# Scores of two heads at once in the two 64-row halves of TensorE, and fillers in one piece

## What is computed

```python
q = (x @ Wq)                       # 32 heads of 16 columns
k, v = x @ Wkv                     # 8 groups; each is shared by 4 heads
scores = q @ k.T                   # per head 1024 x 1024, causal
weights = softmax(scores / 4)      # HD = 16, so 1 / sqrt(HD) is 1/4
x = layernorm(x + (weights @ v) @ Wo + bo)
h = x @ lora_A.T ; lora = h @ (lora_B * coef)      # 8 adapters of rank 16
out = layernorm(x + x @ W.T + bias + lora)
```

## Time and profile before

| | us |
|---|---|
| median of 3 runs | 341.34 |
| lowest and highest | 339.17, 341.63 |
| the profiled execution, whole | 339.0 |
| its span in the trace | 337.2 |

### The profile page before, as it was taken

How to read it: one execution, slowest core, us unless ns; L and a number is a source line. 1 busy time by engine, 2 the same in 40 slices (tenths; PEclk the granted TensorE clock), 3 DMA queues, 4 the chain that set the end, 5 groups by cost and what they waited for, 6 DMA issues and landing times.

```text
span 337.2 us, 7240 instructions
## 1 busy us (share of the span) xinstructions
PE 322.3 (96%) x2487; PEld 169.7 (50%) x2487; DVE 256.6 (76%) x787; ACT 216.5 (64%) x418; POOL 135.3 (40%) x268
## 2 busy tenths in 40 slices
PE   8999989999999999999999999999999999999992
PEld 3676445455353344454444544544544434558882
DVE  3557968978888899888889889888886961047664
ACT  4754737645657796848757668478585786952431
POOL 8845325433547585347222123212141122331553
PEclk9999999999999999999999999999999999999998
DMA  6886494874244120020010100000000000000002
GB/s 202 289 163 170 132 183 120 225 230 118 53 148 155 36 63 5 3 47 3 3 48 33 48 4 3 0 31 3 3 0 3 32 2 1 2 33 1 0 33 93
DMA packets 16643, 22.96 MB, mean 68 GB/s; under 512 B 3232, under 2 KB 10560, under 8 KB 16608
## 3 DMA queue, kind: packets, MB, share of 16 engines
q1 hardware_dynamic: 16608, 22.51, 24.4%
HBM read 16.29 MB, written 6.03 MB: 66 GB/s over the span
## 4 chain that ended last, share of the span: by engine, by line
PE 71%; DMA 7%; DVE 7%; ACT 4%; issue 4%; SPq 3%; POOL 2%; POOLq 0%; DVEq 0%; ACTq 0%
PE PS L1337 18%; PE PS L1195 16%; PE PS L1135 15%; PE PS L1359 15%; DMA QS<-NMR 3%; ACT PB L856 2%; PE PS L1263 2%; PE PS L1255 2%; DVE scrap L917 2%; DVE MX L910 2%; DMA scr_q<-parts 2%; DMA X<-in_L_attn_x_turned_dram 1%; SPq L490 1%; PE PS L1149 1%; SPq L502 1%
## 5 line engine op out<-in xcount | busy, mean ns | idle before, releaser
L856 ACT ACTIVATE PB<-PS 128x512 f32<-128x512 f32 x288 | 155.6, 604 | 59.1 <-PE PS L1359 57.9
L917 DVE CUSTOM_DVE_ANT_0 scrap<-PS,mask 128x128 bf16<-128x128 f32 (+3 forms) x256 | 111.5, 487 | 17.6 <-PE PS L1135 17.1
L1135 PE MATMUL PS<-KS,QS 96*128 96x512 bf16 (+3 forms) x384 | 107.9, 329 | 2.1 <-DVE MX L910 1.0
L1359 PE MATMUL PS<-QS,KS 99*128 99x512 bf16 x288 | 106.2, 381 | 1.8 <-DMA QS<-NMR 1.4
L910 DVE TENSOR_REDUCE MX<-PS 128x1 f32<-128x512 f32 x128 | 81.9, 684 | 12.4 <-PE PS L1135 11.7
L696 POOL TENSOR_SCALAR_AFFINE_SELECT PB<-PB 128x256 f32<-128x256 f32 (+1 forms) x96 | 46.4, 485 | 104.3 <-ACT PB L856 101.2
L1337 PE MATMUL PS<-PB,VX 128*32 128x256 f32 (+1 forms) x1280 | 78.8, 364 | 0.6 <-ACT PB L856 0.3
L1135 PEld LDWEIGHTS PS<-KS,QS 96*128 96x128 bf16 x384 | 32.9, 98 | 49.4 <-issue 13.6
L1337 PEld LDWEIGHTS PS<-PB,VX 128*32 128x32 f32 x1280 | 33.5, 109 | 41.9 <-issue 19.0
L1195 PE MATMUL PS<-XT,WQ 128*128 128x512 f32 x144 | 45.4, 439 | 0.5 <-ACT NMR L744 0.4
L1359 PEld LDWEIGHTS PS<-QS,KS 99*128 99x128 bf16 x288 | 27.5, 98 | 31.4 <-ACT PB L856 7.9
(11 more groups left out here) (93 smaller groups left out, 263.6 us busy)
## 6 DMA issues: line engine op xcount, KB each, us to landing
scr_q<-parts SPq DMA_DIRECT2D x8, 384.0 KB, 4.0
QS<-scr_q SPq DMA_DIRECT2D x15, 192.0 KB, 2.9
X<-in_L_attn_x_turned_dram SPq DMA_DIRECT2D x8, 256.0 KB, 6.3
X<-in_L_attn_x_dram SPq DMA_DIRECT2D x8, 256.0 KB, 3.1
out_dram<-TC SPq DMA_DIRECT2D x8, 256.0 KB, 2.0
QS<-scr_q SPq DMA_DIRECT2D x15, 128.0 KB, 3.0
RAW<-in_L_attn_Wo_dram SPq DMA_DIRECT2D x2, 512.0 KB, 5.9
RAW<-in_L_ffn_W_dram SPq DMA_DIRECT2D x2, 512.0 KB, 9.0
```

What stands on the lines that cost most here:

```text
L856: nc.scalar.activation(PB[:, cyc % NP_BUF, k, :], PS[:, score_bank(e), :], ACT.Exp, scale=SCALE)\
L917: last = nc.vector.tensor_tensor_reduce(out=scrap[:, n % 2, (j - j0) * width:(j - j0 + 1) * width], in0=bank[:, j - j0, :], in1=mask[:, HT ...
L1135: last = nc.tensor.matmul(PS[:, CHUNK_BANK[n], k * width:(k + 1) * width], QS[0:ROWS, u % SLOTS, j, qb * P:(qb + 1) * P], KS[0:ROWS, g, k0 ...
L1359: nc.tensor.matmul(PS[:, score_bank(e), :], KS[0:NROW, u % G, kb * P:(kb + 1) * P], QS[0:NROW, u % SLOTS, heads[0]:heads[-1] + 1, s * HQ + ...
```

## The change

The parts of q and k become two float32r values (high and low) instead of three bfloat16, and a score is three products (48 rows of the array). With the three rows of the maxima that is 51 rows, under 64. So rows 0 to 63 of the array take heads 0 and 1 of a unit, and rows 64 to 127 heads 2 and 3, each with its own keys: the heads are dealt anew, so that a unit has two heads of each of two groups (`v_group`). The two matmuls of a pair have different rows of the array and different PSUM banks, stand behind each other in the queue of PE, and only the second raises the semaphore.

- Scores for exp: a cycle has two `pair_scores` (quarters 0 and 2) instead of four or three `piece_scores`. Both banks must be free before the first matmul. The diagonal has four pieces (two of 256 columns) and four masks.
- Maxima: chunks come in pairs, with both banks free before the first matmul. The planner deals pairs over quarters.
- Fillers, long and short, are issued whole in quarter 3, after its chunks and before `accumulate`.
- ACT has no middle part (L737), POOL and DVE no low third part (L582, L968). `direct` has 2 products instead of 3 and two query matmul groups instead of four.
- The rows of unit 0 go the same way as the others, by `turn_maxima` and a DMA. A unit's rows take two DMAs instead of three, its queries four instead of three, the keys four instead of six.

The core of the diff:

```diff
-    ROWS = 6 * HD
+    ROWS = 3 * HD
     NROW = ROWS + NPART
+    PAIR, TILE = 2, 64
+    Q_TERMS, K_TERMS = (0, 0, 1), (0, 1, 0)
...
-        return first + ([(1, range(0, 4), P)] if on_diagonal(cyc) else [(1, heads, 0) for _, heads, _ in first])
+        return first + [(1, heads, P if on_diagonal(cyc) else 0) for _, heads, _ in first]
...
-        QS = sb("QS", [P, SLOTS, REP, HT], BF16)
-        KS = sb("KS", [P, G, T], BF16)
+        QS = sb("QS", [P, SLOTS, NPAIR, HT], F32R)
+        KS = sb("KS", [P, G // 2, T], F32R)
...
                 was_read(CHUNK_BEHIND[n])
-                for k, j in enumerate(heads):
-                    last = nc.tensor.matmul(PS[:, CHUNK_BANK[n], k * width:(k + 1) * width],
-                                            QS[0:ROWS, u % SLOTS, j, qb * P:(qb + 1) * P],
-                                            KS[0:ROWS, g, k0:k0 + width], start=True, stop=True)
+                was_read(CHUNK_BEHIND[n + 1])
+                for k in range(len(CHUNKS[n][3])):
+                    for t in range(PAIR):
+                        j = CHUNKS[n + t][3][k]
+                        rows = tile_rows(t, ROWS)
+                        last = nc.tensor.matmul(PS[:, CHUNK_BANK[n + t], k * width:(k + 1) * width],
+                                                QS[rows, u % SLOTS, j % NPAIR, qb * P:(qb + 1) * P],
+                                                KS[rows, v // 2, k0:k0 + width], start=True, stop=True)
...
-                long = kind in LONG
-                if not long and head % 2 == 0:
+                if head < 3:
                     return
-                part, parts = (head, REP) if long else (head // 2, 2)
+                part, parts = 0, 1
...
+            def pair_scores(cyc, i):
+                e = SCORE_BANKS[cyc] + PAIR * i
+                for t in range(PAIR):
+                    bank_free(e + t)
+                for t in range(PAIR):
+                    _, heads, skip = pieces(cyc)[PAIR * i + t]
+                    rows = tile_rows(t, NROW)
+                    last = nc.tensor.matmul(PS[:, score_bank(e + t), 0:len(heads) * (HQ - skip)],
+                                            KS[rows, (u % G) // 2, kb * P:(kb + 1) * P],
+                                            QS[rows, u % SLOTS, :, s * HQ + skip:(s + 1) * HQ], start=True, stop=True)
+                last.then_inc(scores, 1)
...
                 for j, lot in enumerate(chunks_of_cycle(cyc)):
-                    for n in lot:
+                    for n in lot[::PAIR]:
                         chunk_scores(n)
-                    if j < len(pieces(cyc)):
-                        piece_scores(cyc, j)
+                    if j % 2 == 0:
+                        pair_scores(cyc, j // 2)
```

More of the change, by code:

```diff
@@ L133, in chunks_of_job @@
         before, due = PLAN_A[n - 1][1] if n else 0, PLAN_A[n][1]
-        a, b = (before + (max(before, due) - before) * p // 3 for p in (part, part + 1))
+        a, b = (before + (due - before) // 2 * p // 3 * 2 for p in (part, part + 1))
         return range(a, b)
@@ L152, in postln_kernel @@
     assert list(FILL) == sorted(FILL)
-    POOL_AT = {c + 1: [("low", PROJ.index(job))] for c, job in FILL.items() if job in PROJ}
+    POOL_AT = {}
     for b in range(TB):
@@ L194, in level @@
             done += r
-            due.append(sum(1 for n in chunks if COST[n + 1] - COST[chunks[0]] <= done + 1))
+            due.append(2 * sum(1 for n in chunks[::2] if COST[n + 2] - COST[chunks[0]] <= done + 1))
         due[-1] = len(chunks)
@@ L275, in postln_kernel @@
     LATE = [(e - WIDE) % ALL_BANKS for e in range(SCORE_BANKS[NCYC - 1], SCORE_BANKS[NCYC])]
-    FREE = [bank for bank in range(ALL_BANKS) if bank not in LATE] + [MISC]
+    FREE = [bank for bank in range(ALL_BANKS) if bank not in LATE] + [MISC, LATE[0]]
+    LATE = LATE[1:]
     assert len(LATE) == 3 and len(FREE) == 4
@@ L1146, in direct @@
             def direct(lhs, slot, bank):
-                for a in range(NPART):
-                    last = nc.tensor.matmul(PS[0:ROWS, bank, :], lhs[:, a, :], parts[:, slot, a, :],
-                                            start=(a == 0), stop=(a == NPART - 1))
+                for a in range(2):
+                    last = nc.tensor.matmul(PS[:, bank, :], lhs[:, a, :], parts[:, slot, a, :], start=(a == 0),
+                                            stop=(a == 1))
                 last.then_inc(moved, 1)
             def direct_keys():
-                pe.wait_ge(parts_ready, 1)
+                pe.wait_ge(*freed(("K", 0, 0)))
                 pe.wait_ge(sel_ready, 12)
@@ L1295, in _ @@
                     pe_job(n, part)
-                    for k in chunks_of_job(n, part):
+                    for k in chunks_of_job(n, part)[::PAIR]:
                         chunk_scores(k)
```

304 lines of the change are left out of this document (133 added, 171 removed).

## The result

The kernel after took **423.1 us** (median of four; 415.5 to 539.6) against 340.6 before (339.2 to 341.6). The profiled execution took 416.1 us with a span of 414.4, against 339.0 and 337.2. I had said 360, with a range of 334 to 376: the direction was right and the size was far off.

What follows compares the result with a forecast made beforehand. PE's own sum was taken to bound B and C (96% and 99% busy), with paired bank waits coming onto the path. Stages A, B, C, D: -2 + 10.8 + 14.3 - 2.2 = +20.9 on 339.0, so 360 us; range 334 to 376.

Steps and rivals of the forecast that it cites:

- The mechanism: Stages B and C: waits for score and chunk banks lengthen cycles, PE and DVE get less busy; 360 us, chance 0.70.
- Its size in C: Stage C, cycles 24 to 70: waits, fillers and switches make it 166.2 us, +14.3 us.
- pair 0 to pair 1: Two score pairs of a cycle: the second leaves 1.13 us after the first, waiting for the first exp's bank.
- three pairs over three banks: Cycles with three chunk pairs sharing three banks: two waits of 1.21 us, cycle length 4.0 us.
- A pair at 0.24: Two row-half matmuls on PE overlap and cost one float32r matmul, 0.24 us; without overlap 0.47.
- 0.12 for a switch: Each further change of the array's split, at every filler and turned row: 0.12 us, 3.4 in C, 1.8 in B.
- A: Stage A, startup and first cycles: shorter startup chain against a DMA for unit 0's rows; -2 us, between -5 and +4.
- B: Stage B, cycles 3 to 23: waits for banks, fillers and switches make it 86.8 us, +10.8 us.
- D: Stage D, six banks, no wait between pairs: PE's saved work less switches gives -2.2 us, between 0 and -3.
- 1 (work sets the stages): Stages B and C: PE fills its pauses and DVE is fed to 93%; 318 us, half of it 329; chance 0.17.
- 2 (no change): Whole kernel: the gain of plain cycles pays for the long ones; about 341 us, chance 0.07.
- 3 (halves do not overlap, 410 us): Row-half pairs on PE take 0.47 us and each wait 0.23 more; about 410 us, chance 0.06.

Runs made afterwards that it cites:

- b_order: Kernel before, bfloat16 matmuls on the whole array, given all of the change's order: paired waits, common semaphores, chunks in pairs, whole fillers; 411.0 us, ratio 1.208.
- b_half_rows: Kernel before with both kinds of score matmuls on rows 0 to 47 only, instructions and waits kept; 382.2, 364.2 and 375.0 us, a fourth execution 803.
- the measured stretch: Kernel before with unread matmuls of several kinds added behind its last output; float32r pairs took 0.24 us, forty matmuls all in one half 14 us instead of 9.4.

## Why the prediction was right and wrong, point by point

**What failed most: the sum has no term for TensorE's clock.** I read 1.00 in the earlier trace rows and carried it over. The change lets PE wait in the fullest cycles and puts matmuls over 51 of 128 rows into every cycle, and the clock falls to 1.2 GHz in stretches; b_order shows the first cause and b_half_rows the second. By the line this is worth 423 - 378 = 45 us on the median, 38 on the profiled execution. Even the 378 lies just outside my range, by the errors in the waits and in stage A below. Such a stretch in B (windows of 2 us, columns as above):

```profile
66.00:68.00 2.00, 1.03 (x6) 0.60 (x6) 1.83 (x8) 1.48 (x4) 0.15 (x1) 1.00 0.04 10
68.00:70.00 2.00, 1.12 (x6) 0.53 (x4) 1.44 (x5) 0.26 (x1) 0.66 (x2) 0.64 0.35 62
70.00:72.00 2.00, 1.33 (x8) 1.10 (x7) 1.92 (x10) 0.66 (x2) 0.76 (x2) 0.50 0.88 300
72.00:74.00 2.00, 2.00 (x6) 1.58 (x5) 0.38 (x4) 0.00 (x0) 0.00 (x0) 0.50 0.97 98
76.00:78.00 2.00, 1.66 (x19) 0.60 (x18) 0.69 (x1) 0.84 (x2) 0.00 (x0) 1.00 1.04 340
```

PE waits for DVE in the fullest cycles, 1.03 to 1.33 us busy of 2, then the whole filler runs at half speed. This cycle, with Q and four pairs, took 11.4 us; I had 8.5 (5.8 + 2.8 + 0.12 - 0.21), and it was 6.4 before. Its like in b_order took 10.6 with its own fall of the clock, and 7.1 with fillers in parts, at 1.00.

**The mechanism was right.** The paired waits set the stages, PE idles ahead of the second score pair for ACT and ahead of chunk pairs for DVE, and DVE got less busy, not more. b_order and the two kernels with a paired wait show that it is the wait (with its common semaphore), not the order of scores. I had worked the walk out for pairs and never asked what own waits would do; two scores at once cost nothing with them, two chunks 5 us.

**Its size in C was off by 12 us at full clock** (estimate: 178 with cycles at 0.5 replaced by their like at 1.0; I had 166).

| cycle of C, full clock | predicted | measured |
|---|---|---|
| pair 0 to pair 1 | 1.13 | 1.28 to 1.34 |
| one or two chunk pairs | 2.70, 2.78 | 2.89 |
| three pairs over three banks | 4.0 | 4.34 |
| the same with T2 or T1b | 4.56 | 4.93, 4.76 |
| three pairs over four banks, with T3 | 4.06 | 4.10 |
| the same with WO | 6.4 | 6.65 |

The first row is the mis-sized term: issue to exp is 0.54 to 0.60 here, not 0.48, and start of the exp to the next pair 0.74, not the 0.65 of the earlier trace rows. It stands in nearly every cycle, once for ACT, and again for DVE where pairs wait for chunk banks.

**A pair at 0.24** was right, and so was 0.12 for a switch (0.09 to 0.14). In place a score pair and the next instruction are 0.30 to 0.34 apart. The Trainium skill's rule that row groups run together ("TensorE: Matmul & The Clock Gate", Part 3) agrees with 0.24. The same part advises one semaphore on the last tile, to save a few tens of ns per tile; here that form, with a wait for both banks and two matmuls over the whole array, cost 14 us twice. Part 1 of that page names the two levels, which the rows show as 1.00 and 0.50, and ties the lower one to an idle engine; in b_half_rows PE is 100% busy at 0.50, and the measurement decides.

**A** went the other way: -2 predicted, +10.9. The rows of unit 0: turned at 35.66, issued from 36.23, and cycle 0's first score leaves at 39.48, where it left at 36.04 before, +3.4 (I had bounded this by 5 and then booked a gain). The other 7.5 lie in cycles 0 to 2, most of them at a clock of 0.50. The order alone makes 5 us of A.

**B**: +31.8 against +10.8. b_order, at a clock of 0.98 over all, has +25.5, and with fillers in parts +13.7, near my number. So the whole fillers in the fullest cycles are what I priced too low: the four with Q take 9.2 to 10.6 us in b_order (at 0.82 to 0.84) and 6.8 to 7.9 with parts, at 1.00. The fall of the clock in just these cycles is part of it.

**D**: no gain. PE's busy time fell by 1.1 us from the earlier trace rows, not by 2.9, at a clock of 0.98.

**PE and DVE in C** I put at 76% and 78%; they are 79% and 71%: DVE's work is the same, C is longer than my sum.

**The rivals.** 1 (work sets the stages): no, nothing is above 81% in B. 2 (no change): no. 3 (halves do not overlap, 410 us) came nearest in time, by luck, and is wrong in cause: they overlap, 0.24.

## What to carry to other kernels

Before tiles are put into parts of the array, ask what stands on the path: here PE's 43 us of saved work (my sum) went into waits for banks and into changes of the split, and even in before's order nothing of it was left. If two tiles go together and banks are few, let each wait for its own bank and raise its own semaphore. And look at the granted clock as a cost of its own, stage by stage: waits before a long run of matmuls and matmuls on half of the rows both brought it down here, and the second cost more through it than it saved.

## What was not expected of the hardware

- The granted clock fell from 1.00 to 0.50 with PE 100% busy when its matmuls used 48 to 51 of the rows, alone (376 to 385 us of the measured stretch) and in a kernel (60 to 100 us of b_half_rows). Why most of stage C keeps 1.00 with the same matmuls stays open.
- It fell to 0.50 also with whole-array matmuls, in the four cycles with Q of b_order, after PE had been busy 0.83 and 1.34 of 2 us in windows waiting for DVE; with fillers in parts the same cycles kept 1.00.
- The same kernel took 415.5 and 539.6 us, at mean clocks of 0.895 and 0.532: how long the stretches last differs from one execution to the next, and so does the time, by far more than in any full-array kernel here (within 2%).
- A change between half-array and full-array matmuls cost 0.09 to 0.14 us. Between half-array scores and the value product, in place in b_half_rows, it cost nothing beyond what full-array scores pay.
